# A Mamba-style mixer in a Trainium2 decoder kernel: later transposes, a gate kept in PSUM, passes over bank pairs, four decay buffers, output weights scaled on ScalarE

## What is computed

```python
proj = einsum('bsd,ed->bse', x, in_proj_w)            # gate | hs, B, C | dt
hBC = silu(causal_depthwise_conv(hBC, conv_w, K=4) + conv_b)
dt = clip(softplus(dt + dt_bias), 0, 100);  A_dt = -exp(A_log) * dt
L = exp(segsum(A_dt))                                  # decay of token s at token l, s <= l
Y = einsum('bzlhn,bzshn,bhzls,bzshp->bzlhp', C, B, L, hs * dt) + hs * D
g = Y * silu(gate)
gg = g * rsqrt(mean(g * g over each of the 8 groups) + 1e-5) * norm_w
x = layernorm(x + einsum('bsi,oi->bso', gg, out_proj_w))
```

## Time and profile before

| what | value |
|---|---|
| median of 3 runs | 2893.6 us (2892.76 to 2895.74) |
| profiled execution: its time, its span | 2891.43 us, 2889.7 us |
| mean granted TensorE clock, of 2.4 GHz | 0.957 |
| mixer's groups | 345 to 1815 us of the span |
| ScalarE evacuation of 512 columns (L1015), mean | 777 ns |
| ScalarE high half of a gated tile (L1037), mean | 631 ns |
| GpSimd low half of a weight (L1100), min / median / max | 1255 / 1328 / 3282 ns |
| GpSimd score product of 1024 (L1123), min / median / max | 2366 / 2409 / 4408 ns |
| VectorE scan of 1024 (L1219), min / median / max | 2258 / 2605 / 4089 ns |
| VectorE gate multiply of 512 (L1243), min / median / max | 691 / 1120 / 2520 ns |
| VectorE sum over 8 tiles (L1251), mean | 2004 ns |

### The profile page before, as it was taken

One profiled execution on the slowest core, in us unless ns is written; L12 is line 12 of the kernel. 1 busy time (PEld: TensorE's weight loads), 2 busy tenths in 40 slices (PEclk: granted clock), 3 DMA queues, 4 the chain that ended last, 5 costly groups with the idle time before them and its releaser, 6 DMA issues. The chain is left out here.

```text
span 2889.7 us, 43136 instructions
## 1 busy us (share of the span) xinstructions
PE 2588.2 (90%) x14376; PEld 2111.7 (73%) x14376; DVE 1901.5 (66%) x2844; ACT 1085.0 (38%) x2329; POOL 1331.9 (46%) x902
## 2 busy tenths in 40 slices
PE   7877499999999999999999999699999999999958
PEld 4435377777777777777777777588888888888846
DVE  4554399597896977969779697364544645546453
ACT  2221233333333333333333433254544544545431
POOL 3000177596785866858669587222122122221210
PEclk9888799999999999999999999799999999999989
DMA  3000223132240322303223030201000000000010
GB/s 139 1 0 1 70 99 114 34 121 62 82 128 23 127 68 80 108 27 132 80 78 110 26 132 23 62 19 30 18 22 29 18 22 22 21 29 18 12 51 30
DMA packets 87731, 163.75 MB, mean 57 GB/s; under 512 B 9424, under 2 KB 10064, under 8 KB 87312
## 3 DMA queue, kind: packets, MB, share of 16 engines
q1 hardware_dynamic: 85408, 158.15, 16.7%
q10 hardware_dynamic: 2160, 3.43, 0.4%
HBM read 158.92 MB, written 2.62 MB: 56 GB/s over the span
## 5 line engine op out<-in xcount | busy, mean ns | idle before, releaser
L157 PE MATMUL bank<-XH,d_w_hi 128*128 128x512 f32 x1160 | 475.1, 410 | 81.2 <-POOL d_w_lo L1100 57.8
L159 PE MATMUL bank<-XH,d_w_lo 128*128 128x512 f32 x1160 | 460.9, 397 | 0.0
L158 PE MATMUL bank<-XL,d_w_hi 128*128 128x512 f32 x1160 | 459.6, 396 | 0.0
L1219 DVE TENSOR_TENSOR_SCAN d_decay<-d_decay,m_delta 128x1024 f32<-128x1024 f32 x128 | 348.0, 2756 | 49.3 <-DMA d_decay<-token_decays 34.8
L1123 POOL TENSOR_TENSOR d_decay<-d_decay,d_cb 128x1024 f32<-128x1024 f32 x128 | 352.0, 2768 | 57.6 <-DVE d_decay L1219 48.5
L1100 POOL TENSOR_TENSOR d_w_lo<-d_w,d_w_hi 128x512 fp32r<-128x512 f32 x144 | 276.6, 1922 | 120.4 <-ACT d_w_hi L994 120.4
L157 PEld LDWEIGHTS bank<-XH,d_w_hi 128*128 128x128 f32 x1160 | 221.1, 191 | 146.2 <-issue 66.6
L1201 DVE SCALAR_TENSOR_TENSOR d_hs<-bank,d_conv,d_hs 128x508 f32<-128x508 f32 (+2 forms) x384 | 277.6, 737 | 10.4 <-ACT d_hs L1015 1.4
L159 PEld LDWEIGHTS bank<-XH,d_w_lo 128*128 128x128 f32 x1160 | 221.4, 191 | 49.8
L158 PEld LDWEIGHTS bank<-XL,d_w_hi 128*128 128x128 f32 x1160 | 221.9, 191 | 44.4
L1129 POOL TENSOR_TENSOR d_gated_lo<-d_gated,d_gated_hi 128x512 fp32r<-128x512 f32 x128 | 165.5, 1296 | 167.2 <-ACT d_gated_hi L1037 167.2
(11 more groups left out here) (275 smaller groups left out, 6398.9 us busy)
## 6 DMA issues: line engine op xcount, KB each, us to landing
d_decay<-token_decays SPq DMA_DIRECT2D x128, 512.0 KB, 4.8
d_w<-in_L_w_groups SPq DMA_DIRECT2D x144, 256.0 KB, 3.1
e_w<-in_L_w_heads SPq DMA_DIRECT2D x80, 256.0 KB, 2.6
d_wo<-in_L_wo_groups SPq DMA_DIRECT2D x64, 256.0 KB, 4.9
X<-in_x SPq DMA_DIRECT2D x8, 256.0 KB, 11.0
b_ctx<-in_ctx SPq DMA_DIRECT2D x8, 256.0 KB, 11.5
e_ctx<-in_ctx SPq DMA_DIRECT2D x8, 256.0 KB, 2.8
out<-X SPq DMA_DIRECT2D x8, 256.0 KB, 2.0
```

The costliest lines, as they stand in the source:

```text
L157: pe.matmul(out, wh, xh, start=first, stop=False)
L158: pe.matmul(out, wh, xl, start=False, stop=False)
L159: return pe.matmul(out, wl, xh, start=False, stop=last)
L1219: v.tensor_tensor_scan(r, r, m["DELTA"][:], 0.0, ALU.mult, ALU.add).then_inc(q["decay"], 1)
```

## The change

TensorE's PSUM becomes four pairs of banks: IN (banks 0, 1: hs and B), Y (2, 3: B times C, scores times hs), TURN (4, 5: turned hs; the output product), GATES (6, 7: C and the gates). Passes of ScalarE and VectorE over hs, gate, y, the mask and the turned hs cover 1024 tokens at once; only the evacuation, taps and silu of B and C stay in halves. The gate's silu is written back to its own banks, and the multiply reads them there. hs j + 1 is projected before hs j is transposed. The decay rows have four buffers, one load of 1 MB for each j; B and C share the third buffer, and the squares share the tile of the dt product. ScalarE scales the output weights. SP issues the next group's weights 1 to 4 before that group's first rows. The order of the weight tiles on the host follows.

```diff
+RSLOT = 4
+BC_SLOT = 2
-        self.bank = [ctx.enter_context(nc.psum_tensor(f"bank{i}", [P, 512], F32)) for i in range(8)]
+        self.pair = [ctx.enter_context(nc.psum_tensor(f"pair{i}", [P, 1024], F32)) for i in range(4)]
+        self.bank = [self.pair[i // 2][:, (i % 2) * 512:(i % 2 + 1) * 512] for i in range(8)]
...
-        R = sb("d_decay", [P, 2, 2, 2, HALF])
+        R = sb("d_decay", [P, RSLOT, 2, T])
+        BC = R[:, BC_SLOT, :, :]
-        SQ, SQS = sb("d_sq", [P, JT, S]), sb("d_sq_sum", [P, 2, S])
+        SQ, SQS = XDT, sb("d_sq_sum", [P, 2, S])
...
+        IN, GATES, Y, TURN = c.pair[0], c.pair[3], c.pair[1], c.pair[2]
+        def hs_item(j):
+            return 2 * j + 1 if j else 2
+        def gate_item(j):
+            return 2 * j + 4 if j < JT - 1 else LPG - 1
...
@@ block.sync @@
-                def group(g):
-                    weight(g, 0)
-                    weight(g, 1)
+                def group(g, last_group=False):
                     for j in range(JT):
-                        weight(g, 2 + 2 * j)
-                        weight(g, 3 + 2 * j)
-                        sp.wait_ge(q["y_ready"], START + 2 * (g * JT + j - 1))
-                        for h in range(2):
-                            sp.dma_start(R[:, j % 2, h, :, :], rows[bass.ds(g, 1), j, :, tokens(h)]
-                                         .broadcast_to([P, 2, HALF])).then_inc(rows_in[j % 2][h], 16)
+                        if j == BC_SLOT:
+                            sp.wait_ge(q["cb_ready"], START + g + 1)
+                        else:
+                            sp.wait_ge(q["y_ready"], START + g * JT + j - RSLOT + 1)
+                        sp.dma_start(R[:, j % RSLOT, :, :].rearrange("p h t -> p (h t)"),
+                                     rows[bass.ds(g, 1), j, :].broadcast_to([P, 2 * T])
+                                     ).then_inc(rows_in[j % RSLOT], 16)
                         for i in WO_AFTER.get(j, ()):
...
+                        for i in (2 * j + 5, 2 * j + 6) if j < JT - 1 else (LPG + 1, LPG + 2, LPG + 3, LPG + 4):
+                            if i < LPG or not last_group:
+                                weight(g, i)
+                for i in range(5):
+                    weight(0, i)
...
@@ block.tensor, project @@
+                    if i == 0:
+                        pe.wait_ge(q["tap"], START + 3 * g * NU)
+                    elif i == 1:
+                        pe.wait_ge(q["gated"], START + g * JT)
+                    elif i in GATE_OF and GATE_OF[i] == 0:
+                        pe.wait_ge(q["tap"], START + 3 * (g * NU + units(1)[-1] + 1))
+                    elif i in GATE_OF:
+                        pe.wait_ge(q["gated"], START + g * JT + GATE_OF[i])
+                    else:
+                        before = HS_OF[i] - 1
+                        last_unit = units(hs_item(before))[-1] if before >= 0 else units(0)[-1]
+                        pe.wait_ge(q["tap"], START + 3 * (g * NU + last_unit + 1))
...
@@ block.tensor, group @@
                     for j in range(JT - 1):
-                        project(g, 4 + 2 * j)
+                        project(g, hs_item(j + 1))
+                        turn_hs(g, j)
+                        project(g, gate_item(j))
                         scan(g, j)
-                        project(g, 5 + 2 * j)
-                        turn_hs(g, j + 1)
+                    turn_hs(g, JT - 1)
+                    project(g, gate_item(JT - 1))
+                    scan(g, JT - 1)
                     if not last_group:
                         project(g + 1, 0)
-                    scan(g, JT - 1)
-                    if not last_group:
                         project(g + 1, 1)
                         project(g + 1, 2)
-                        project(g + 1, 3)
                         cb(g + 1)
-                        turn_hs(g + 1, 0)
                     out(g, last_group)
...
@@ block.scalar @@
                 def wo_hi(g, i):
+                    act.wait_ge(wo_in[i % 2], 16 * (g * (JT // 2) + i // 2 + 1))
...
+                    act.activation(WOR[:, i % 2, :], WOR[:, i % 2, :], ACT.Copy,
+                                   scale=PN[:, i:i + 1]).then_inc(q["wo_scaled"], 1)
                     act.wait_ge(q["wo_scaled"], START + g * JT + i + 1)
...
                 def gate(g, j):
-                    for h in range(2):
-                        act.wait_ge(q["gate_ready"], START + g * (2 * JT) + 2 * j + h + 1)
-                        act.wait_ge(q["gated"], START + 2 * (g * JT + j - 1))
-                        act.activation(GATE[:, j % 2, tokens(h)], proj_bank(3, h)[:, :], ACT.Silu).then_inc(q["gate"], 1)
+                    act.wait_ge(q["gate_ready"], START + g * JT + j + 1)
+                    act.activation(GATES[:, :], GATES[:, :], ACT.Silu).then_inc(q["gate"], 1)
...
                     for j in range(JT - 1):
+                        w_hi(g, 2 * j + 5)
+                        evac(g, hs_item(j + 1))
+                        if 2 * j + 6 < LPG or not last_group:
+                            w_hi(g, 2 * j + 6)
                         for k in WO_AFTER.get(j + 1, ()):
                             wo_hi(g, k)
+                        silu(g, hs_item(j + 1))
+                        gate(g, j)
                     if not last_group:
                         w_hi(g + 1, 1)
+                    gate(g, JT - 1)
+                    if not last_group:
+                        w_hi(g + 1, 2)
                         evac(g + 1, 0)
                         w_hi(g + 1, 3)
+                        silu(g + 1, 0)
                     gated_hi(g, 0)
                     if not last_group:
+                        evac(g + 1, 1)
+                        w_hi(g + 1, 4)
                         silu(g + 1, 1)
+                        evac(g + 1, 2)
+                    gated_sq(g, 0)
+                    if not last_group:
                         silu(g + 1, 2)
...
@@ block.gpsimd @@
-                    pool.tensor_tensor(WOR[:, i % 2, :], WOR[:, i % 2, :], PN[:, i:i + 1].broadcast_to([P, D]),
-                                       ALU.mult).then_inc(q["wo_scaled"], 1)
...
                     for j in range(JT - 1):
+                        w_lo(g, 2 * j + 5)
+                        if j:
+                            scores(g, j, 1)
+                        scores(g, j + 1, 0)
+                        if 2 * j + 6 < LPG or not last_group:
+                            w_lo(g, 2 * j + 6)
                         for k in WO_AFTER.get(j + 1, ()):
+                            wo_lo(g, k)
                     if not last_group:
                         w_lo(g + 1, 1)
+                    scores(g, JT - 1, 1)
...
@@ block.vector @@
                     for j in range(JT - 1):
-                        decay(g, j + 1)
-                        conv(g, 4 + 2 * j)
-                        gated(g, j)
-                        xdt(g, j + 1)
+                        if j:
+                            gated(g, j - 1)
+                        decay(g, j + 1, 0)
+                        xdt(g, j)
+                        conv(g, hs_item(j + 1))
+                        decay(g, j + 1, 1)
+                    gated(g, JT - 2)
+                    xdt(g, JT - 1)
                     if not last_group:
-                        decay(g + 1, 0)
+                        decay(g + 1, 0, 0)
+                        decay(g + 1, 0, 1)
                         tables(g + 1)
-                        conv(g + 1, 0)
                     gated(g, JT - 1)
                     if not last_group:
+                        conv(g + 1, 0)
                         conv(g + 1, 1)
+                        v.wait_ge(q["skip"], START + (g + 1) * JT)
+                        skip_table(g + 1)
                         conv(g + 1, 2)
-                        v.wait_ge(q["skip"], START + 2 * (g + 1) * JT)
-                        skip_table(g + 1)
                         cb_mask(g + 1)
-                        xdt(g + 1, 0)
                     acc(g, last_group)
```

More of the change, by code:

```diff
@@ L899, in cb @@
-                def cb(g):
-                    pe.wait_ge(q["silu"], START + g * (2 * NCONV) + 4)
-                    pe.wait_ge(q["skip"], START + 2 * g * JT)
-                    for h in range(2):
-                        for b in range(4 * h, 4 * h + 4):
-                            last = pe.matmul(c.bank[2 + h][:, (b % 4) * S:(b % 4 + 1) * S],
-                                             BC[:, 0, b * S:(b + 1) * S], BC[:, 1, b * S:(b + 1) * S],
-                                             start=True, stop=True)
-                        last.then_inc(q["cb_ready"], 1)
@@ new lines, in cb @@
+                def cb(g):
+                    pe.wait_ge(q["silu"], START + g * NU + 4)
+                    pe.wait_ge(q["skip"], START + g * JT)
+                    for b in range(NB):
+                        last = pe.matmul(Y[:, b * S:(b + 1) * S], BC[:, 0, b * S:(b + 1) * S],
```

(14 more changed lines are left out.)

281 lines of the change are left out of this document (125 added, 156 removed).

## The result

| kernel | median, range of runs | ratio to before, 95% interval |
|---|---|---|
| before | 2893.6 us | 1 |
| changed | 2861.1 us (2857.3 to 2862.7) | 0.9885 (0.9868 to 0.9902) |
| forecast | 2864 us (2842 to 2889) | |

The change makes the kernel 32 us faster. Ratios are of executions at a mean granted clock of 0.944 to 0.960; one of e6's five took 3652.1 us at 0.662 and is in no ratio. The profiled execution took 2862.7 us, span 2860.1. The page, where the earlier trace rows stood before: busy us (share of the span) and instructions, and three groups with mean ns of one.

What follows compares the result with a forecast made beforehand. VectorE was taken to pace the loop's turn at 14.68 us, against TensorE's 14.0. Seven periods -31.2, head +8.4, tail -5.2 gave -28.0 from 2891.4, so 2863.4, stated as 2864 us; range 2842 to 2889.

Steps and rivals of the forecast that it cites:

- The walk through VectorE's turn: Loop over j: VectorE's work per turn, pass by pass, falls from 14.68 to 12.1 us and fits TensorE's 14.0.
- rival A: Loop: VectorE still sets the turn through blocking, 15.2 us a turn, 2931 us in all; chance 0.14 together with D.
- D: Loop: pair passes cost what two did, 1.47 us each, so turns take 15.0; its chance lies in rival A's.
- B: Between groups: decay rows land 3 us later, seven times, giving 2885 us; chance 0.13.
- the dearer PSUM source: VectorE passes: a rule of 120 fixed cycles instead of 58, some 0.06 us more per pass, turn 12.2.
- Output weights on ScalarE: Loop: GpSimd loses a product of 1.0 to 1.5 us per item, ScalarE gains about 0.7; costs nothing.
- Four decay buffers: Row loads: SP runs some 8 us ahead in the loop; no gain in the turn, no help between groups.
- Between groups: From one group's loop to the next: late rows cost 3.9 us; the whole period goes from 183.1 to 179.0.
- the wait before P(1): Between groups: TensorE idles 2.9 us before the next group's second projection, waiting for the last gated tile.
- The late reduce: Between groups: the first sum of squares ends after the first output product, 1.1 us lost.
- Head: Start of the stage: first scan product of hs comes at 387.6 instead of 379.17 us, 8.4 lost.
- Tail: Last group: output starts 99.2 us after its first scan product instead of 104.4, 5.2 gained.

Runs made afterwards that it cites:

- e6: Changed kernel, but each row load waits as if there were two decay buffers, though four stay: 2880.3 us, ratio 0.9960.
- e4: Kernel before, with only the scaling of the output weights moved from GpSimd to ScalarE: 2856.6 us, ratio 0.9880.
- e9: Changed kernel with output weights scaled on GpSimd again and ScalarE's rounding of them placed behind the silus: 2907.6 us, ratio 1.0057.
- e7: Changed kernel with output weights scaled on GpSimd again, ScalarE's rounding staying ahead of the silus: 2973.8 us, ratio 1.0285.
- e0: Changed kernel run once more, unaltered: 2864.2 us, ratio 0.9903 to the kernel before.
- e3: Changed kernel with the next group's first decay rows loaded earlier, ahead of its item 3 weight: 2855.6 us, ratio 0.9870.
- e5: As e3, plus half of the next group's first projection done before the last gate projection: 2838.1 us, ratio 0.9814.

## Why the prediction was right, and where it was not

The number was met for the reasons given in part, and in part by luck: the bound was read rightly, the gain of the weights' move was not seen, and between the groups two errors cancelled.

**Bound.** Right: VectorE paced the turn of the kernel before, and with its passes paired TensorE paces it at 14.00, the 14.0 of the forecast. The walk through VectorE's turn holds row by row: skip 1.28 and multiply 1.22 (2.55 forecast), first scan held and over 6.1 after the start of P (6.55), dt product 1.22 (1.21), taps 3.86 (3.8), second scan 2.28 (2.26). Neither rival A nor D happened, nor B: VectorE waited 4.53 for the rows where 4 were forecast. One reading left something out and changed nothing: the turns of 14.01 in the kernel before are not turns in which VectorE kept up. VectorE took 14.7 through the one shown in the earlier trace rows, and 14.9 through the second turn of a group, where TensorE took 14.0 in all eight groups. In every group one longer turn on TensorE, the third (15.8 to 19.1), makes up for it.

**PSUM passes.** The trace has 1221 ns for the multiply with one input in PSUM and the earlier trace rows 1225 with both in SBUF; the dearer PSUM source, which the forecast weighed, does not show.

**Output weights on ScalarE.** Failed: "It costs nothing; the cover is ScalarE's idle time" was said of the cost and no gain was given. The scaling took 712 ns, as said. But alone it gives the kernel before 1.2% (e4), and without it the changed kernel is 0.57% slower than before even with a good order (e9), 2.9% slower with its own (e7). It did not disturb the sum, as the turn that I walked had GpSimd without it. The gain is not in TensorE's turn, which is 14.0 in e9 too, but behind the loop, where the forecast has no price for it.

**Four decay buffers.** Failed: "At no wait it gains nothing in the turn." With the waits of two, a period is 1.8 longer (e6): TensorE's turn is the same, as said, but what VectorE and GpSimd lose in it is paid behind the loop.

**Between groups.** The period was forecast at 179.0 and came out at 178.4, out of partly other terms. Right: the row load 2.7 us after Y(6) (3 forecast), gated(7) done 16.9 after it (16.9), C at 29.0 (29.2); over the seven groups C has a mean of 29.2. Missed: the last gate projection waits 2.0 for gated(6), since in that turn no hs projection stands before it. As TensorE then comes later, the wait before P(1) is 0.58 and not 2.9; in the six groups where the projection ran at the slower clock next to nothing is left of it. Two errors of one chain cancel, which is luck: the end was set by VectorE either way. Seen whole, Y(0) to Y(7) fell from 103.1 to 96.1, and Y(7) to the next Y(0) rose from 80.0 to 82.3. The late reduce cost 0.57 (1.1 forecast).

**Head.** 10.0 and not 8.4; 1.3 of it is that the stage began later in this execution (first load at 341.56 and not at 340.22). Counted from that load, 8.6 were lost, and 8.6 in e0 too. **Tail.** 101.1 after Y(0), 99.2 forecast: 1.7 of it is the missed wait again.

**Sum.** Periods 1248.5 against 1281.5, so -33.0 (-31.2 forecast); head +10.0, tail -3.4: -26.4 (-28.0). The span shrank by 29.6; the other 3.2 lie behind the start of the output product, where the executions of this study differ by that much (1121 to 1125 us from there to the end).

Not tried: the pair passes and the later transposes by themselves on the kernel before, and the repairs of e3 and e5 on top of e4; so it stays open whether the rest of the change is needed for 2833.

## What to carry to other kernels

An instruction that waits for another engine costs what is queued behind it: when work moves between engines, place the waiting instruction behind everything that others need, and test the order by itself (81 us here). A loop that runs at one engine's pace can hide another that falls behind by 0.3 us a turn; look for the debt behind the loop's end. When a change has several parts, time each alone on the old kernel too: here one edit of five was as fast as all of them.

## What the runs showed of the hardware

Written back to PSUM by ScalarE, a silu of 1024 took 1007 ns, and 1058 in SBUF. Which of two instructions of VectorE and GpSimd is held depends on who starts first: in the changed kernel the scan (3.57, score product 2.40), in e9 GpSimd's low half (3.30, scan 2.46). VectorE's gap before the dt product is 0.56 in the one and 1.84 in the other. Where its loop turns, TensorE stood 1.6 to 2.3 us in every run, in most cases with nothing that the profile shows to wait for. A row load of 1 MB landed in 4.8 us at the median, as those of 512 KB had.
